# One more group of tiles turned by VectorE instead of TensorE, with its neighbours in the order moved

## The chip, the core and the metric

The kernel runs on one core of a Trainium2 chip. A core has TensorE for matrix products (and transposes, as products with the identity), VectorE, ScalarE and GpSimd for elementwise work, and SyncE, which issues all transfers here. The metric is the device time of one execution in microseconds.

## The reference

Two graph layers on x (16 graphs of 1024 nodes, 256 features, float32) with an int32 adjacency of 1024 x 1024 for each graph:

```
h = relu(layernorm(x));  Q, K, V = h Wq + bq, h Wk + bk, h Wv + bv   (8 heads of 32)
A = softmax(where(adj == 0, -inf, Q K^T / sqrt(32)));   x = x + (A V) Wo + bo
h = relu(layernorm(x));  e_k = leaky_relu((h * a_k) h^T, 0.2)   for k = 0..3
s = where(adj == 1, e_0, -9e15); where(adj == 2, e_1, s); ...;  x = x + softmax(s) h
```

With the inputs given, the adjacency holds only 0 and 1, so only e_0 is ever chosen; the kernel has branches for the other kinds that are skipped here.

## The kernel before

**Stages, slots, groups.** One stage handles the attention of one graph b, and in its background the second layer of graph b - 1 and the front of graph b + 1 (its norm, transposes, query and key products). There are 16 stages: stage 0 and stage 15 are written out, 1 to 14 are one loop. A stage has 64 slots, one for each tile: tile t = 4g + h is head h of a half of the heads, with 128 query rows; g is the group, 0 to 15, and four tiles make a group. Each engine has its own program, written in the order of the slots, and all meet by counters (semaphores). An engine runs its program strictly in order.

**What a tile needs.** TensorE makes the scores into `ps` (L1205, three slots ahead), VectorE adds the mask and takes the row minimum (L870, two slots ahead), ScalarE takes the exponential in place in `sm` (L595, one slot ahead), then the tile has to be transposed, 128 x 1024, and the four transposed tiles of a group are multiplied by V (`values`, L1236).

**Two ways to transpose.** In a *plain* tile TensorE makes eight 128 x 128 transposes into `pT` (L1217) and ScalarE and VectorE copy a half each into a home in `pt` (L606, L894). In a *swapped* group (`SWAPPED`, groups 3 to 9 before) tiles h = 0 and 1 are *turned*: VectorE transposes their 32 x 32 blocks into `turned` (L882), SyncE sends the blocks to a bounce buffer in HBM by eight transfers and back into homes 0 and 1 of `pt` by two (`swap_blocks`, L333 to L345). Tiles 2 and 3 of such a group stay plain, and ScalarE copies both halves (L606, L610). `turned` lies where the query and key weights lie; these are parked in `ks` at the start and brought back by `restore` (four transfers, L325) once a stage, after the last exchange and before the next front's query products.

**Homes.** `pt` has five. `place(t)` gives the home of a tile, `edge_place(t)` that of a row tile of the second layer. One edge tile, `SPARED` (6 before), lives in `spare`, which shares its memory with `parts`.

**The background.** `background` lists by slot the products that share the banks `pG`: values, edge products, edge sums, front transposes, query and key products. TensorE waits before each until the product two places earlier in that list is evacuated (`released`). The second layer has eight row tiles: two edge products in slots 13 + 4t and 14 + 4t (L1150 with `parts`), the masks of VectorE (L993), leaky relu (L1001), ScalarE's exponential (L655), TensorE's transposes `edge_transposes` (L1283) in slot 16 + 4t, the copies (L660, L1009) and the sums with h (L1292), then `result` (L1017).

**The masks.** SyncE loads a mask row tile as two halves `adj_half` (L279); GpSimd makes the bias of it (L505 for the next graph, L522 for the second layer), and ScalarE counts in `most_kind` (L630) whether other kinds occur, in slots 43, 46, 48, 51, 55, 58 and 61 for the next graph. `most_kind` waits for both halves, and the next load waits for it. On ScalarE it stands in the middle of everything else.

**The front.** VectorE takes statistics (L781), aggregates (L787), GpSimd raises to the power -1/2 (L528), VectorE makes the shift (L837), ScalarE normalises in four pieces (L644, slots 41 to 44). Query and key products go to `parts`, from which `first_stacks` sends twelve transfers (L299) for each of key and query.

Of the kernel before, what the change touches and what calls it, by code (L numbers as in the profile page):

```python
# [14 lines left out]
P = 128  # L15
B, N, D, H = 16, 1024, 256, 8
HD = D // H
NT = N // P
KT = D // P
HG = P // HD  # L20
# [14 lines left out]
SWAPPED = tuple(range(3, 10))  # L35
# [3 lines left out]
SPARED = SWAPPED[-1] + 1 - (EDGE // HG + 1)  # L39
LATE = tuple(t for t in range(NT) if EDGE // HG + 1 + t in SWAPPED)  # L40
# [20 lines left out]
def result_slot(t):  # L61

    return EDGE + 1 + 4 * NT if t == NT - 1 else EDGE + (8 if t in LATE else 7) + 4 * t

# [43 lines left out]
def place(t):  # L108


    g, h = t // HG, t % HG
    if g in SWAPPED:
        return h
    return 3 + (g + 1) % 2 if h == 0 else h - 1
# [12 lines left out]
def two_graph_layers(nc, x, adj, wq, bq, wk, bk, wv, bv, wo, bo, a_cols, y):  # L127
    ctx = ExitStack()
    with ctx:
# [98 lines left out]
        g_a, g_e, g_sel, g_chain = sem("g_a"), sem("g_e"), sem("g_sel"), sem("g_chain")  # L228
        def edge_home(t, c):

            if t == SPARED:
                return spare[:, c, 0:HALF].rearrange("p (m n) -> p m n", n=P)
            return pt[:, edge_place(t), NT // 2 * c:NT // 2 * (c + 1), :]
# [20 lines left out]
        def _(sp):  # L254
# [48 lines left out]
            def first_stacks(f, q):  # L303

                sp.wait_ge(qk_h, 8 * f + 2 * q + 2)
                settle(sp)
                sp.wait_ge(qk_l, 8 * f + 2 * q + 2)
                settle(sp)
                for head in range(HG):
                    stack(head, q)  # L310
# [58 lines left out]
            def stage(b, later):  # L369
# [34 lines left out]
                store(o, 4)  # L404
                if later:
                    mask_adj(b + 1, 0, base)
                    restore(b)
# [13 lines left out]
                if later:  # L421
                    mask_adj(b + 1, 3, base)
                    first_stacks(b + 1, 0)
                    mask_adj(b + 1, 4, base)
                    first_stacks(b + 1, 1)
                    mask_adj(b + 1, 5, base)
                    mask_adj(b + 1, 6, base)
# [33 lines left out]
            for t in range(NT - 1):  # L461
                if t == 1:
                    swap_blocks(0, 9)
                    restore(0)
                if t == 1:
                    sp.wait_ge(f_tr, 8)
                    settle(sp)
                    load_x1(0)
                sp.wait_ge(most_made, NT + t)
                settle(sp)  # L470
                load_adj(1, t, NT + t)
                if t == 3:
                    first_stacks(1, 0)
                if t == 4:
                    first_stacks(1, 1)
# [16 lines left out]
        def _(pool):  # L492
# [48 lines left out]
            def stage(b, later):  # L541
                o, base = b - 1, LOADS * b
                next_masks(b, NT - 1)
                layer_rstd(o)
                for t in range(NT):
                    if later and t == NT - 1:
                        front_rstd(b + 1)
                    edge_bias(o, t, base + t, NT * (b + 1))
                if later:
                    for node in range(5):  # L550
                        next_masks(b + 1, node)
                residual(b)
                if later:
                    for node in range(5, NT - 1):
                        next_masks(b + 1, node)
# [20 lines left out]
        def _(act):  # L576
# [21 lines left out]
            def copy(b, t, first):  # L598
                act.wait_ge(tr[0], len(PLAIN) * b + plain_before(t) + 1)
                if t % HG and (t >= HG or not first):  # L600
                    act.wait_ge(av, GROUPS * b + t // HG)
# [4 lines left out]
                nc.scalar.copy(pt[:, place(t), 0:NT // 2, :], pT[0][:, :].rearrange("p (m n) -> p m n", n=P)  # L606
                               ).then_inc(pt_made[0], 1)
                if t // HG in SWAPPED:
                    act.wait_ge(tr[1], len(PLAIN) * b + plain_before(t) + 1)
                    nc.scalar.copy(pt[:, place(t), NT // 2:, :], pT[1][:, :].rearrange("p (m n) -> p m n", n=P)  # L610
                                   ).then_inc(pt_made[1], 1)
# [51 lines left out]
            def stage(b, earlier, later):  # L663
# [36 lines left out]
                for s in range(TILES):  # L700
# [24 lines left out]
                    if later and s in (41, 42, 43, 44):  # L725
                        front_norm(b + 1, s - 41)
# [37 lines left out]
        def _(dve):  # L764
# [121 lines left out]
            def copy(b, t, first):  # L886
                dve.wait_ge(tr[1], len(PLAIN) * b + plain_before(t) + 1)
                if t % HG and (t >= HG or not first):
                    dve.wait_ge(av, GROUPS * b + t // HG)
# [4 lines left out]
                nc.vector.tensor_copy(pt[:, place(t), NT // 2:, :],  # L894
# [125 lines left out]
            def stage(b, earlier, later):  # L1020
# [26 lines left out]
                for s in range(TILES):  # L1047
                    for t in range(NT - 1):
                        if earlier and s == result_slot(t):
                            result(o, t, pG[bank("sum", t)])  # L1050
                    if s + 2 < TILES:
# [7 lines left out]
                    if earlier and EDGE + 4 <= s < EDGE + 4 + 4 * NT and (s - EDGE) % 4 == 0:  # L1059
                        t = (s - EDGE - 4) // 4  # L1060
                        edge_copy(o, t)
# [10 lines left out]
                    for kind, n in ahead[s]:  # L1072
                        if kind == "edge":
                            evacuate(kind, n)
                    if s in TURNED:
# [16 lines left out]
                    if later and s in (34, 38, 39):  # L1092
                        for n in {34: (3,), 38: (2,), 39: (0, 1)}[s]:
                            front_stats(b + 1, n)
                    if later and s == 40:
                        front_aggregate(b + 1)
                        front_shift(b + 1)
# [39 lines left out]
        def _(pe):  # L1137
# [83 lines left out]
            def values(b, g, i):  # L1221
# [7 lines left out]
                for m in range(NT):  # L1229
                    for h in range(HG):  # L1230
# [3 lines left out]
                        else:  # L1234
                            moving = pt[:, place(HG * g + h), m, :]
# [235 lines left out]
```

## Time and profile before

| | |
|---|---|
| median of 3 runs | 3695.5 us (3694.56 to 3705.17) |
| the profiled execution | 3700.19 us, its span 3698.4 us |
| granted clock of TensorE, mean | 0.972 of full |
| TensorE matmul, weight load | 3289.2 us (89%), 2715.2 us (73%) |
| VectorE, ScalarE, GpSimd | 2818.1 us (76%), 2448.6 us (66%), 1112.7 us (30%) |
| transfers of SyncE's queue | 538.36 MB, 52.9% of 16 engines' span |
| VectorE's copy of half a plain tile (L894) | 576 of them, mean 686 ns |

A busy share is an average over the whole span. Matmul records overlap, so the mean of one (279 ns for a 128 x 128 transpose) is longer than its part of the time: eight in a row take about 0.9 us from the first start to the next instruction's. In a timeline the bracket at the end of a line gives how long the engine stood idle just before and what ended it.

### The profile page before, as it was taken

What the parts mean: (1) busy time and instruction counts of PE and PEld (TensorE: products, weight loads), DVE (VectorE), ACT (ScalarE), POOL (GpSimd) and SP (SyncE); (2) the same over time, 40 slices, a digit from 0 to 9 for tenths busy, and PEclk for the clock granted to TensorE, in tenths of its full rate; (3) what the DMA queues carried; (4) which work ended last, traced back from release to release, by engine and by line L of the source; (5) the groups of instructions that cost most, each with busy time, mean ns of one, the idle gap of its engine ahead of it and who ended that gap; (6) DMA issues with size and microseconds to landing.
All of it is one profiled execution on the core that took longest, in us unless ns stands there. A gap on an engine that the chain in (4) does not pass through costs nothing. (4 is left out here: it accounts for less than half of the span.)

```text
span 3698.4 us, 96789 instructions
## 1 busy us (share of the span) xinstructions
PE 3289.2 (89%) x32304; PEld 2715.2 (73%) x32304; DVE 2818.1 (76%) x5398; ACT 2448.6 (66%) x4548; POOL 1112.7 (30%) x568
## 2 busy tenths in 40 slices
PE   5789989999998999999998998999999999998975
PEld 4577777777777787777777777777777777777854
DVE  4678777787878878777787878778787787877752
ACT  4677766767667677766767667676666767676641
POOL 1232323324223342322324233242322324232212
PEclk9899999999999999999999999999999999999987
DMA  5745546465454755546475454646545475554511
GB/s 132 207 123 156 159 124 180 127 197 139 134 168 122 206 136 167 153 122 173 128 209 144 130 170 125 194 130 177 150 130 166 123 212 143 156 160 113 157 33 39
DMA packets 331133, 546.84 MB, mean 148 GB/s; under 512 B 44480, under 2 KB 209600, under 8 KB 328384
## 3 DMA queue, kind: packets, MB, share of 16 engines
q1 hardware_dynamic: 330432, 538.36, 52.9%
q8 instruction: 334, 5.47, 0.6%
q14 instruction: 367, 3.01, 0.3%
HBM read 286.53 MB, written 134.22 MB: 114 GB/s over the span
## 5 line engine op out<-in xcount | busy, mean ns | idle before, releaser
L870 DVE CUSTOM_DVE_ANT_0 sm<-ps,bias 128x1024 f32<-128x1024 f32 x1024 | 1246.3, 1217 | 72.4 <-issue 28.5
L595 ACT ACTIVATE sm<-sm,mn 128x1024 f32<-128x1024 f32 x1024 | 1179.2, 1152 | 82.1 <-DVE mn L870 81.2
L1217 PE MATMUL pT<-ident,sm 128*128 128x128 f32 x6400 | 867.5, 279 | 147.3 <-ACT pt L606 111.0
L1217 PEld LDWEIGHTS pT<-ident,sm 128*128 128x128 f32 x6400 | 732.7, 142 | 327.6 <-ACT pt L606 159.7
L606 ACT COPY pt<-pT 128x512 f32<-128x512 f32 x800 | 465.1, 581 | 642.6 <-PE pT L1217 500.1
L522 POOL TENSOR_SCALAR gbias<-adj_half 128x512 bf16<-128x512 int32 x256 | 492.8, 1925 | 1195.3 <-DVE mn L993 906.4
L1205 PE MATMUL ps<-ks,qs 96*128 96x512 f32 x2048 | 752.5, 449 | 86.4 <-DVE mn L870 82.7
L505 POOL TENSOR_SCALAR bias<-adj_half 128x512 bf16<-128x512 int32 x256 | 492.5, 1924 | 785.6 <-DMA adj_half<-in_adj_dram 729.0
L894 DVE COPY pt<-pT 128x512 f32<-128x512 f32 x576 | 395.3, 686 | 267.0 <-PE pT L1217 200.9
L1236 PE MATMUL pG<-pt,v 128*32 128x128 f32 x16384 | 529.6, 284 | 26.3 <-DVE pt L894 19.6
L1236 PEld LDWEIGHTS pG<-pt,v 128*32 128x32 f32 x16384 | 456.0, 114 | 109.6 <-issue 87.7
L1205 PEld LDWEIGHTS ps<-ks,qs 96*128 96x128 f32 x2048 | 348.3, 193 | 185.0 <-DVE mn L870 143.1
L1292 PE MATMUL pG<-h,pt 128*128 128x256 f32 x1680 | 409.2, 379 | 0.0
L1150 PE MATMUL pG<-hh,parts 128*128 128x512 f32 x1024 | 382.6, 416 | 9.2 <-DVE x L1017 6.5
L993 DVE CUSTOM_DVE_ANT_0 sm<-pG,gbias 128x512 f32<-128x512 f32 x256 | 176.6, 690 | 219.0 <-PE pG L1150 174.0
L1292 PEld LDWEIGHTS pG<-h,pt 128*128 128x128 f32 x1680 | 308.7, 189 | 43.4
L882 DVE STREAM_TRANSPOSE turned<-sm 128x1024 f32<-128x1024 f32 x224 | 277.8, 1240 | 0.0
L655 ACT ACTIVATE sm<-sm,mnl 128x1024 f32<-128x1024 f32 x128 | 146.9, 1148 | 156.0 <-DVE mnl L1004 155.9
L1150 PEld LDWEIGHTS pG<-hh,parts 128*128 128x128 f32 x1024 | 199.2, 195 | 61.0 <-DVE x L1017 16.6
L1283 PE MATMUL pT<-ident,sm 128*128 128x128 f32 x1024 | 143.4, 286 | 83.0 <-ACT sm L655 66.1
L1150 PE MATMUL pG<-hh,wqk 128*128 128x512 f32 x512 | 192.9, 419 | 14.4 <-DVE hl L795 8.0
L1150 PE MATMUL pG<-hl,parts 128*128 128x512 f32 x512 | 205.6, 402 | 0.0
(102 smaller groups left out, 3617.6 us busy)
## 6 DMA issues: line engine op xcount, KB each, us to landing
adj_half<-in_adj_dram SPq DMA_DIRECT2D x512, 256.0 KB, 3.6
bounce<-turned SPq DMA_DIRECT2D x896, 128.0 KB, 2.5
pt<-bounce SPq DMA_DIRECT2D x224, 512.0 KB, 4.6
ks<-parts SPq DMA_DIRECT2D x384, 128.0 KB, 2.6
qs<-parts SPq DMA_DIRECT2D x384, 128.0 KB, 2.8
x<-in_x_dram SPq DMA_DIRECT2D x16, 1024.0 KB, 5.8
out_dram<-x SPq DMA_DIRECT2D x128, 128.0 KB, 4.6
wqk<-ks SPq DMA_DIRECT2D x60, 256.0 KB, 4.7
```

The lines of the kernel that those rows point to most:

```text
L505: nc.gpsimd.tensor_scalar(bias[:, node, c * HALF:(c + 1) * HALF], adj_half[:, c, :], 0.0, BIG, ALU.is_equal, ALU.mult).then_inc(adj_used[c ...
L522: nc.gpsimd.tensor_scalar(half, adj_half[:, c, :], 0.5, BIG, ALU.is_lt, ALU.mult).then_inc(adj_used[c], 1)
L595: nc.scalar.activation(sm[:, ring(t), :], sm[:, ring(t), :], ACT.Exp, scale=-1.0, bias=mn[:, t:t + 1], accum_out=den[:, t:t + 1]).then_inc ...
L606: nc.scalar.copy(pt[:, place(t), 0:NT // 2, :], pT[0][:, :].rearrange("p (m n) -> p m n", n=P)).then_inc(pt_made[0], 1)
L870: nc.vector.tensor_tensor_reduce(out=sm[:, ring(t), :], in0=ps[t % 2][:, :], in1=bias[:, node, :], scale=1.0, scalar=3e38, op0=ALU.add, op ...
L882: nc.vector.transpose(turned[:, t % HG, :, :, :].rearrange("p c m j -> p m c j"), sm[:, ring(t), :].rearrange("p (m c j) -> p m c j", m=NT ...
L894: nc.vector.tensor_copy(pt[:, place(t), NT // 2:, :], pT[1][:, :].rearrange("p (m n) -> p m n", n=P)).then_inc(pt_made[1], 1)
L1150: last = nc.tensor.matmul(out, a, c, start=start and i == 0, stop=stop and i == len(terms) - 1)
L1205: last = nc.tensor.matmul(ps[t % 2][:, c * HALF:(c + 1) * HALF], qs[0:ROWS, head, node * P:(node + 1) * P], ks[0:ROWS, head, c * HALF:(c + ...
L1217: last = nc.tensor.transpose(pT[c][:, j * P:(j + 1) * P], sm[:, ring(t), m * P:(m + 1) * P], ident[:, :])
L1236: last = nc.tensor.matmul(pG[i][HD * h:HD * (h + 1), 0:P], v[:, m, o:o + HD], moving, start=(m == 0), stop=(m == NT - 1))
L1292: last = nc.tensor.matmul(out[:, 0:D], edge_home(t, m // 4)[:, m % 4, :], h1[:, m, :], start=(m == 0), stop=(m == NT - 1))
```

## The change

`SWAPPED` becomes 3 to 10, so tiles 40 and 41 are turned too. From it follow: `SPARED` becomes 7, `LATE` gains edge tile 6, and the values of group 10 move from behind slot 44 to ahead in slot 46. Tile 45 (`ASIDE`) would take home 0 while group 10's exchanged tile is there, so it gets a home of its own beside the spared edge tile (`tile_home`). The parity in `place` follows the last swapped group. The front's statistics, aggregate and shift on VectorE and its norm on ScalarE are spread a slot later; the power on GpSimd comes behind the last edge bias instead of ahead of it. SyncE exchanges group 10, then restores the weights, then loads the first mask of the next graph, which stood ahead of the restore; and the query stacks are sent two heads before the sixth mask load and two behind it.

SyncE, after the exchange of group 9, in the loop (bounce and pt<-bounce are an exchange, wqk<-ks the restore, adj_half the mask). Before:

```order
L345 DMA pt<-bounce 128x1024 [waits bounced1]
L357 ISA [waits y_made]
L357 DMA out_dram<-x 128x256
L291 ISA
L279 ISA [waits g_sel,adj_used0]
L279 DMA adj_half<-in_adj_dram 128x512
L279 ISA [waits adj_used1]
L279 DMA adj_half<-in_adj_dram 128x512
L350 REGISTER_ALU
L325 DMA wqk<-ks 32x2048 [waits bounced0,bounced1]
L325 DMA wqk<-ks 32x2048 x3
```

Now:

```order
L344 DMA bounce<-turned 32x4x256 [waits turn_made]
L344 DMA bounce<-turned 32x4x256 x3
L348 REGISTER_ALU
L353 DMA pt<-bounce 128x1024 [waits bounced0,av]
L353 DMA pt<-bounce 128x1024 [waits bounced1]
L358 REGISTER_ALU
L333 DMA wqk<-ks 32x2048 [waits bounced0,bounced1]
L333 DMA wqk<-ks 32x2048 x3
L299 ISA
L287 ISA [waits g_sel,adj_used0]
L287 DMA adj_half<-in_adj_dram 128x512
L287 ISA [waits adj_used1]
```

The mask load moved from ahead of the restore to behind an exchange and the restore.

ScalarE, from the norm in slot 43 to tile 44's copy, before (gbias,most is the mask count, mnl the exponential of edge 7):

```order
L644 ACTIVATE rb<-rb,nmr,rstd 128x256
L625 REGISTER_ALU
L630 ACTIVATE gbias,most<-adj_half,mhalf 128x1024 [waits l_masked,adj_in1,adj_in0]
L594 REGISTER_ALU
L595 ACTIVATE sm,den<-sm,mn 128x1024 [waits masked]
L654 ISA
L655 ACTIVATE sm,den<-sm,mnl 128x1024 [waits leaky]
L599 REGISTER_ALU
L605 REGISTER_ALU [waits av,tr0]
L606 COPY pt<-pT 128x512 [waits pv]
```

Now:

```order
L655 ACTIVATE x<-x,nmr,rstd 128x256 [waits f_nmr]
L655 ACTIVATE x<-x,nmr,rstd 128x256
L636 REGISTER_ALU
L641 ACTIVATE gbias,most<-adj_half,mhalf 128x1024 [waits l_masked,adj_in1,adj_in0]
L605 REGISTER_ALU
L606 ACTIVATE sm,den<-sm,mn 128x1024 [waits masked]
L665 ISA
L666 ACTIVATE sm,den<-sm,mnl 128x1024 [waits leaky]
L610 REGISTER_ALU
L616 REGISTER_ALU [waits av,tr0]
L617 COPY pt<-pT 128x512 [waits pv]
```

Only the piece that is normalised ahead of it is another (x for rb). The mask count keeps its slot, and everything for slot 44 is still behind it.

TensorE, slots 44 to 46. Before, the values of group 10 stood in slot 44 ahead of the first front transposes (ident,x):

```order
L1205 MATMUL ps<-ks,qs 128x512 x2
L1214 REGISTER_ALU
L1217 MATMUL pT<-ident,sm 128x128 x8
L1236 MATMUL pG<-pt,v 32x128 x32
L1317 REGISTER_ALU
L1154 ISA
L1157 MATMUL pG<-ident,x 128x128 x4
L1389 REGISTER_ALU
L1283 MATMUL pT<-ident,sm 128x128 x8
L1368 REGISTER_ALU
```

Now the values stand in slot 46, ahead of the sum of edge tile 7 (h,spare), which the last front transposes (ident,sq) follow at once:

```order
L1250 MATMUL pG<-pt,v 32x128 x32
L1228 REGISTER_ALU
L1231 MATMUL pT<-ident,sm 128x128 x8
L1333 REGISTER_ALU
L1306 MATMUL pG<-h,spare 128x256 x8
L1315 REGISTER_ALU
L1168 REGISTER_ALU
L1171 MATMUL pG<-ident,rb 128x128 x4
L1168 REGISTER_ALU
L1171 MATMUL pG<-ident,sq 128x128 x4
```

The values moved two slots back, and the sum of edge tile 7 now touches the last front transposes.

```diff
-SWAPPED = tuple(range(3, 10))
+SWAPPED = tuple(range(3, 11))
+ASIDE = HG * (SWAPPED[-1] + 1) + 1
-    return EDGE + 1 + 4 * NT if t == NT - 1 else EDGE + (8 if t in LATE else 7) + 4 * t
+    return EDGE + 2 + 4 * NT if t == NT - 1 else EDGE + (8 if t in LATE else 7) + 4 * t
-    return 3 + (g + 1) % 2 if h == 0 else h - 1
+    assert t != ASIDE
+    return 3 + (g + SWAPPED[-1]) % 2 if h == 0 else h - 1
+        def tile_home(t, c):
+            if t == ASIDE:
+                return spare[:, 2 + c, 0:HALF].rearrange("p (m n) -> p m n", n=P)
+            return pt[:, place(t), NT // 2 * c:NT // 2 * (c + 1), :]
...  SyncE, in the loop
                 swap_blocks(b, 9)
                 store(o, 4)
+                swap_blocks(b, 10)
                 if later:
+                    restore(b)
                     mask_adj(b + 1, 0, base)
-                    restore(b)
...
-                    first_stacks(b + 1, 1)
+                    first_stacks(b + 1, 1, range(2))
                     mask_adj(b + 1, 5, base)
+                    first_stacks(b + 1, 1, range(2, HG))
                     mask_adj(b + 1, 6, base)
...  GpSimd
                 for t in range(NT):
-                    if later and t == NT - 1:
-                        front_rstd(b + 1)
                     edge_bias(o, t, base + t, NT * (b + 1))
+                if later:
+                    front_rstd(b + 1)
...  ScalarE
-                    if later and s in (41, 42, 43, 44):
-                        front_norm(b + 1, s - 41)
+                    if later and s in (42, 43, 44, 45):
+                        front_norm(b + 1, s - 42)
...  VectorE
+                    if earlier and s == EDGE + 4 + 4 * SPARED:
+                        edge_copy(o, SPARED)
+                    if later and s == 42:
+                        front_shift(b + 1)
-                    if later and s in (34, 38, 39):
-                        for n in {34: (3,), 38: (2,), 39: (0, 1)}[s]:
-                            front_stats(b + 1, n)
-                    if later and s == 40:
+                    if later and s in (34, 38, 39, 40):
+                        front_stats(b + 1, {34: 3, 38: 2, 39: 0, 40: 1}[s])
+                    if later and s == 41:
                         front_aggregate(b + 1)
-                        front_shift(b + 1)
...  ScalarE and VectorE, copy
-                if t % HG and (t >= HG or not first):
+                if t % HG and t != ASIDE and (t >= HG or not first):
```

## Rows read from the trace of the kernel before

**Rows 1.** Groups by form: line, engine, operation, shapes, count, busy us, mean ns, idle before.

```profile
L595 ACT ACTIVATE sm<-sm,mn 128x1024 f32<-128x1024 f32 x1024 | 1179.2, 1152 | 82.1 <-DVE mn L870 81.2
L1217 PE MATMUL pT<-ident,sm 128*128 128x128 f32 x6400 | 867.5, 279 | 147.3 <-ACT pt L606 111.0 <-issue 29.4 <-ACT pt L660 5.0
L606 ACT COPY pt<-pT 128x512 f32<-128x512 f32 x800 | 465.1, 581 | 642.6 <-PE pT L1217 500.1 <-PE pG L1236 128.6 <-PE pG L1292 13.8
...
L644 ACT ACTIVATE x<-x,nmr,rstd 128x256 f32<-128x256 f32 x64 | 34.9, 598 | 11.5 <-DVE nmr L837 11.5
```

**Rows 2.** Timeline of TensorE: start us, duration us, instruction [idle before <- what ended it].

```profile
1669.72 0.71 PE L1205 MATMUL ps<-ks,qs 96*128 96x512 f32 x2
...
1682.47 0.71 PE L1205 MATMUL ps<-ks,qs 96*128 96x512 f32 x2
...
1719.88 0.75 PE L1205 MATMUL ps<-ks,qs 96*128 96x512 f32 x2
...
1729.39 1.06 PE L1217 MATMUL pT<-ident,sm 128*128 128x128 f32 x8 [2.06 <-issue]
...
1742.60 1.95 PE L1236 MATMUL pG<-pt,v 128*32 128x128 f32 x64
...
1744.98 1.04 PE L1283 MATMUL pT<-ident,sm 128*128 128x128 f32 x8
...
1755.88 0.49 PE L1150 MATMUL pG<-hh,wqk 128*128 128x512 f32 x1 [0.48 <-DVE hl L795]
...
1792.32 1.36 PE L1217 MATMUL pT<-ident,sm 128*128 128x128 f32 x8 [2.22 <-ACT pt L606]
```

**Rows 3.** Timeline of GpSimd: the powers of front (L528) and layer (L539).

```profile
1064.76 1.66 POOL L528 TENSOR_TENSOR rstd<-vpe,mhalf 128x8 f32<-128x8 f32 x1 [18.89 <-DVE vpe L790]
1163.15 1.67 POOL L539 TENSOR_TENSOR rstd<-vpe,mhalf 128x8 f32<-128x8 f32 x1 [11.43 <-DVE vpe L833]
...
1725.10 1.66 POOL L528 TENSOR_TENSOR rstd<-vpe,mhalf 128x8 f32<-128x8 f32 x1 [18.89 <-DVE vpe L790]
1824.61 1.67 POOL L539 TENSOR_TENSOR rstd<-vpe,mhalf 128x8 f32<-128x8 f32 x1 [13.89 <-DVE vpe L833]
...
2168.83 1.66 POOL L528 TENSOR_TENSOR rstd<-vpe,mhalf 128x8 f32<-128x8 f32 x1 [18.89 <-DVE vpe L790]
2265.54 1.67 POOL L539 TENSOR_TENSOR rstd<-vpe,mhalf 128x8 f32<-128x8 f32 x1 [12.22 <-DVE vpe L833]
```

**Rows 4.** Timeline of VectorE at slots 37, 39 and 40.

```profile
1713.28 1.24 DVE L882 STREAM_TRANSPOSE turned<-sm 128x1024 f32<-128x1024 f32 x1
...
1721.02 1.40 DVE L781 BATCH_NORM_STATS2 st<-x 128x6 f32<-128x256 f32 x4
...
1726.79 0.17 DVE L837 SCALAR_TENSOR_TENSOR nmr<-mv,rstd 128x8 f32<-128x8 f32 x1 [1.88 <-POOL rstd L528]
```

**Rows 5.** Timeline of ScalarE: the mask counts of slots 43 and 58.

```profile
1739.81 1.14 ACT L630 ACTIVATE gbias<-adj_half,mhalf 128x1024 bf16<-128x1024 int32 x1
...
1789.43 1.15 ACT L630 ACTIVATE gbias<-adj_half,mhalf 128x1024 bf16<-128x1024 int32 x1 [1.81 <-DMA adj_half<-in_adj_dram]
```

**Rows 6.** Timeline of SyncE's transfer issues: start us, duration of all issues, count.

```profile
1717.55 1.64 SPq L345 DMA_DIRECT2D pt<-bounce  x2
...
1731.59 3.56 SPq L325 DMA_DIRECT2D wqk<-ks  x4
...
1776.22 8.69 SPq L299 DMA_DIRECT2D qs<-parts  x12
1785.41 1.39 SPq L279 DMA_DIRECT2D adj_half<-in_adj_dram  x2
```

**Rows 7.** Stretches: us, busy of PE, PEld, DVE, ACT, POOL, clock, transfers.

```profile
1792.00:1796.00 4.00, 3.68 (x56) 3.17 (x60) 2.58 (x4) 2.46 (x5) 2.54 (x3) 0.63 0.62 178
2081.00:2090.00 9.00, 6.98 (x24) 5.13 (x28) 7.05 (x16) 5.61 (x10) 0.92 (x1) 0.62 0.76 232
```

**Rows 8.** Issues of the page: count, KB each, median us from issue to landing.

```profile
adj_half<-in_adj_dram SPq DMA_DIRECT2D x512, 256.0 KB, 3.6
```

More of the change, by code:

```diff
@@ L301, in stack, with first_stacks @@
                                  ).then_inc((k_stacked, q_stacked)[q][head], 16)
-            def first_stacks(f, q):
+            def first_stacks(f, q, heads=range(HG)):
                 sp.wait_ge(qk_h, 8 * f + 2 * q + 2)
@@ L308, in first_stacks @@
                 settle(sp)
-                for head in range(HG):
+                for head in heads:
                     stack(head, q)
@@ L463, in _ @@
                     swap_blocks(0, 9)
+                    swap_blocks(0, 10)
                     restore(0)
@@ L605, in copy @@
                     act.wait_ge(pv, NT * b - NT + AFTER_SUM.index(t) + 1)
-                nc.scalar.copy(pt[:, place(t), 0:NT // 2, :], pT[0][:, :].rearrange("p (m n) -> p m n", n=P)
+                nc.scalar.copy(tile_home(t, 0), pT[0][:, :].rearrange("p (m n) -> p m n", n=P)
                                ).then_inc(pt_made[0], 1)
@@ L609, in copy @@
                     act.wait_ge(tr[1], len(PLAIN) * b + plain_before(t) + 1)
-                    nc.scalar.copy(pt[:, place(t), NT // 2:, :], pT[1][:, :].rearrange("p (m n) -> p m n", n=P)
+                    nc.scalar.copy(tile_home(t, 1), pT[1][:, :].rearrange("p (m n) -> p m n", n=P)
                                    ).then_inc(pt_made[1], 1)
@@ L887, in copy @@
                 dve.wait_ge(tr[1], len(PLAIN) * b + plain_before(t) + 1)
-                if t % HG and (t >= HG or not first):
+                if t % HG and t != ASIDE and (t >= HG or not first):
                     dve.wait_ge(av, GROUPS * b + t // HG)
@@ L893, in copy @@
                     dve.wait_ge(pv, NT * b - NT + AFTER_SUM.index(t) + 1)
-                nc.vector.tensor_copy(pt[:, place(t), NT // 2:, :],
+                nc.vector.tensor_copy(tile_home(t, 1),
                                       pT[1][:, :].rearrange("p (m n) -> p m n", n=P)).then_inc(pt_made[1], 1)
@@ L1060, in stage @@
                         t = (s - EDGE - 4) // 4
-                        edge_copy(o, t)
+                        if t != SPARED:
+                            edge_copy(o, t)
                     if earlier and s == 2:
@@ L1234, in values @@
                         else:
-                            moving = pt[:, place(HG * g + h), m, :]
+                            moving = tile_home(HG * g + h, m // 4)[:, m % 4, :]
                         last = nc.tensor.matmul(pG[i][HD * h:HD * (h + 1), 0:P], v[:, m, o:o + HD], moving, start=(m == 0), stop=(m == NT - 1))
```

## The prediction

> **What bounds the kernel now.** I read the page first, then the groups by form, then GpSimd's timeline for the length of a stage, then TensorE's timeline through one stage, and last the timelines of VectorE, SyncE and ScalarE around each place where TensorE stood still. TensorE is busy 89% of the span, and the weight loads beside it 73%. The largest TensorE group is the transposes of the exponentials: 6400 of them [rows 1]. Between slots 16 and 39 TensorE does not stop: slot 24 begins at 1669.72 and slot 28 at 1682.47, so a turned group takes 12.75 us of pure TensorE work [rows 2]. What TensorE loses lies at three kinds of place, the same in every stage:
> - In slots 40 to 47 it waits six times, 5.0 us together (1.15, 2.06, 0.70, 0.27, 0.36, 0.48). The longest is 2.06 us at 1729.39 [rows 2]. It is labelled "issue", but the copy it needs from VectorE is behind the shift of the front's norm, and VectorE waits 1.88 us there for GpSimd's power [rows 3, 4].
> - In slot 60 it waits 2.22 us at 1792.32 for a ScalarE copy [rows 2]. ScalarE is late because at 1789.43 it waited 1.81 us for the sixth mask tile [rows 5]. That load was issued at 1785.41, right after twelve stack transfers that held SyncE for 8.69 us from 1776.22 [rows 6].
> - Lower clock: after that second wait the granted clock is 0.63 over 1792 to 1796 [rows 7]. From the front's power to the layer's power a stage takes 96.71 us where no clock drop falls in it, 98.39 with only one near slot 41, 99.51 with only one near slot 60 [rows 3]. So a drop costs about 1.7 and 2.8 us. In 3 us slices of the trace the first is there in ten of the 14 stages and the second in nine, on average 1.2 and 1.8 us a stage.
>
> **Sum, part by part.** All times are those of the stage whose front power is at 1725.10, where no clock drop falls at slot 41. I work the new schedule from 1719.88, where slot 40 begins [rows 2], with durations from start to start.
>
> *Fewer transposes.* Tiles 40 and 41 leave TensorE: 16 transposes. Eight take about 0.87 us from start to start, so 1.75 us a stage, all of it on the path. By the ends of its rows it could be 2 x 8 x 0.279 = 4.5 us, since the listed 279 ns overlap; I take 1.75 [rows 1]. ScalarE keeps four copies (tiles 42 and 43, both halves). VectorE loses four copies of 0.69 (the table of the profile) and gains two transposes of 1.24 [rows 4], nothing on balance.
>
> *VectorE up to the turn.* The front's statistics stood as four in a row at 1721.02 [rows 4]; now two of them stand there (0.7), then mask 42 (1.15), turn 40 (1.15, to 1724.0), two statistics (0.7), result 5 (0.55), mask 43 (1.15, to 1726.4), the copy of edge 6 (0.6), edge mask 14 (0.6), turn 41 (1.15) to 1728.8, and the aggregate. The power needs from 1725.10 to 1726.79 as before [rows 3, 4], so the shift now comes at 1731.5. The copy that stood behind it is now before it. The 2.06 us wait becomes one of 1.2 us, at the scores of slot 42 (they need mask 43), and the 1.15, 0.70 and 0.27 go. TensorE then runs slot 42 from 1726.5: scores, values of group 9, transposes, edge 15, a quarter of edge values to 1731.9; slot 43 to 1734.1; slot 44's scores, transposes (behind a copy, 1734.9), half an edge value and the first front transposes to 1737.85. There it stands at the transposes of edge 7, which in the kernel before began at 1744.98 [rows 2]. Up to here the change is 7.1 us ahead: this is what it would give if nothing took it back.
>
> *What takes it back.* These transposes need ScalarE's exponential of edge 7 and its copy of tile 44, and both are queued behind the mask count of slot 43, which reads the first mask tile of the next front. On SyncE that load now stands behind the exchange of group 10 and behind the four transfers that restore the weights; before, it stood ahead of both. The chain: turn 41 ends 1728.8. For group 9 the turn of tile 37 ended at 1714.44 (1713.28 plus 1.16), and the two loads back were issued by 1719.19 (1717.55 plus 1.64), 4.75 us after it [rows 4, 6]. So SyncE is free at 1733.55. The restore takes 3.56 to issue [rows 6]: 1737.4. The halves of the mask follow, the second at about 1738.3, and land 3.6 us later [rows 8]: 1741.9. ScalarE reaches the count at 1735.8: shift 1731.5, two norms 1.0, exponential 44 1.15, two copies 1.0, two norms 1.0 [rows 1]. Before, it started the count at 1739.81 without a wait [rows 5]. Now it waits some 6 us, then needs count 1.14, exponential 45 1.14, exponential of edge 7 1.14, copy 0.5, a start 0.2: TensorE goes on at 1746.1, after 8.2 us of standing. For the load's arrival I take both ends: 2.8 us if nothing is queued in front of it (1741.1), 4.7 us, as the restore's own pieces need (1743.0), and 3.6 as the middle.
>
> A rule of the Trainium skill bears on this, page "DMA: Bandwidth & Descriptors", section "Queues, rings and completion order": on each engine the descriptors of one issuing queue are consumed in ring order, though a later one can finish first. By that rule the mask waits for the restore's megabyte, which speaks for the late end, about 1 us a stage more than my value. No row here shows this order of transfers.
>
> *Slots 45 to 47.* The work from edge 7's transposes to the first query product took 1744.98 to 1755.88, 10.9 us, of which 0.84 were waits [rows 2]. The values of group 10 now stand in it, 64 records from 1742.60, 1.95 us long and 1.89 to the next start [rows 2], and the last front transposes need result 7, which now comes directly behind sum 7: 0.6 us. With 0.1 to 0.3 for others, 10.06 + 1.89 + 0.6 = 12.5. The query product begins at 1758.6, that is 2.7 us late.
>
> *Clock.* After 8 us of standing I expect the lower clock (1.2 GHz) in every stage, where waits of 2.06 us had it in ten of 14. A lower-clock stretch in this trace costs 1.7, 2.8 and, over 2081 to 2090 at 0.62, 9 x 0.38 = 3.4 us [rows 3, 7]. I take 2.5; the drop near slot 41 that it replaces gave 1.2. Net +1.3. The Trainium skill, "TensorE: Matmul & The Clock Gate", Part 1, says that the throttled state is the default and activity releases it; by that rule the drop is certain here, as in my sum, and no run yet shows it.
>
> *Stacks.* Only six query transfers now stand before the sixth mask (heads 0 and 1), so it is issued half of 8.69 = 4.3 us earlier by SyncE, limited by GpSimd's release to about 3.9. It lands near 1785.5, and ScalarE asks at 1787.6 [rows 5, 6]. The 1.8 us wait goes, and with it 1.8 of TensorE's 2.22. The other six transfers end by 1787, long before slot 61 needs them. The clock drop near slot 60 goes with it: 1.8 on average. The wait of 1.65 us for the fifth mask, behind the key stacks, stays.
>
> *Homes.* Other places in pt, the spare home for tile 45 and edge 7: same instructions and sizes. Nothing, bounds -0.2 to +0.2 us a stage, because only the order of waits changes.
>
> Sum a stage: +2.7 + 1.3 - 1.8 - 1.8 = +0.4. Over 14 looped stages +6 us; the first and last stage have no such load behind a restore and give 1.75 each, -4. Profiled: 3700.2 + 2 = 3702. The median shown is 4.7 below the profiled run, so 3698.
>
> **Rivals.**
> 1. *The load is in time.* If the mask tile lands at or before 1735.8, TensorE continues at 1739.9 and not 1746.1 and keeps its clock: 0.4 - 6.2 - 2.5 = -8.3 a stage, 14 x 8.3 = 116, with the 4 of the outer stages 120, time 3576. It needs 6 us less on a chain of issues that are all in the trace. Half of it, a load 3 us earlier at the same clock, is 0.4 - 3.1 = -2.7 a stage and gives 3653. For it: the stores and exchange can be faster here, since fewer loads run beside them. Against: every issue has its row. Chance 0.20 for 3576 to 3660.
> 2. *The standing costs more clock than I give it (slower).* Place: slots 44 to 47 behind edge 7. If TensorE is at the lower level from its restart up to the query product, more than 5 us, it costs the 3.4 us of 2081 to 2090 and not 2.5, and with the load at 4.7 us (+1.1) the stage is +2.4, 14 x 2.4 = 34, less 4: 3725. If in addition the next stretch drops again (2.8) it is +5.2: 3765. It decides from a standing of about 10 us, or from two low stretches a stage. Chance 0.20.
> 3. *The change is hidden.* Slots 40 to 47 are bound by ScalarE and SyncE and not by TensorE, the stack gain is eaten by the load for slot 61: within 3 us of before, 3695. Chance 0.05.
>
> **How the numbers follow.** The forecast, 3698, has 0.55, own range 3665 to 3735: 1 us more or less on the load and 1 us on the clock are 14 us each, and either of the two gains can fail by half. Of it 0.17 is faster by over 0.3% (11 us, about what a measurement of this kernel tells from no change), 0.19 within, 0.19 slower. With rival 1 faster has 0.37, with rival 3 the middle 0.24, with rival 2 slower 0.39. The range reaches to half of either rival: 3625 to 3750.
>
> **What would show it.** Right: ScalarE's count of slot 43 waits some 5 to 7 us for adj_half in each looped stage, TensorE's transposes of edge 7 wait some 8 us with a clock near 0.5 behind them, VectorE's wait for the power is under 1 us and holds nobody, the sixth mask has no wait and the clock is 1.00 in slots 60 to 62. TensorE has 6144 transposes on that line. Wrong: no wait at that count (rival 1), or a waiting adj_half at slot 58 still (the stack term is lost, +3.6 a stage).

## The result, and the profile after

The changed kernel takes 3810.89 us (median of 4 runs, 3798.64 to 3816.13), the kernel before 3695.03 on the same chip (3693.89 to 3705.17): 1.0303 times, interval 1.027 to 1.0335. It is slower by 3%, outside the predicted range. The profiled execution took 3816.13 us, its span is 3814.3, the mean granted clock 0.947 after 0.972.

The page after: TensorE, the transposes of the exponentials, those of the second layer, ScalarE's mask counts, the instruction queue, and the landing of masks and restored weights.

```profile
PE 3286.5 (86%) x32048; PEld 2714.4 (71%) x32048; DVE 2819.8 (74%) x5366; ACT 2446.3 (64%) x4548; POOL 1112.7 (29%) x568
...
q8 instruction: 345, 5.65, 0.7%
...
L1231 PE MATMUL pT<-ident,sm 128*128 128x128 f32 x6144 | 839.3, 280 | 71.7 <-ACT pt L617 68.7
...
L1297 PE MATMUL pT<-ident,sm 128*128 128x128 f32 x1024 | 157.9, 305 | 234.0 <-ACT pt L617 170.3
...
L641 ACT ACTIVATE gbias<-adj_half,mhalf 128x1024 bf16<-128x1024 int32 x128 | 146.7, 1146 | 170.0 <-DMA adj_half<-in_adj_dram 168.1
...
adj_half<-in_adj_dram SPq DMA_DIRECT2D x512, 256.0 KB, 4.1
...
wqk<-ks SPq DMA_DIRECT2D x60, 256.0 KB, 6.9
```

The 256 transposes are gone from the first group ([rows 1] had 6400), and its own idle time has halved. It has gone elsewhere: 170.3 us before the transposes of the second layer, and 168.1 us of ScalarE waiting for masks. One instruction queue moved 345 pieces; in the page of before this row reads `334, 5.47, 0.6%`, for a longer TensorE program. The prediction does not use that row.

TensorE in the stage whose front power is at 2011.00, and its jump back to the loop's top in the stage before (start, duration, instruction, [idle before]).

```profile
1860.57 1.09 PE L1231 MATMUL pT<-ident,sm 128*128 128x128 f32 x8 [0.32 <-ACT pt L617]
1864.86 1.19 PE L1219 MATMUL ps<-ks,qs 96*128 96x512 f32 x2 [3.20 <-issue]
...
2001.19 0.75 PE L1219 MATMUL ps<-ks,qs 96*128 96x512 f32 x2
...
2007.78 0.73 PE L1219 MATMUL ps<-ks,qs 96*128 96x512 f32 x2 [1.08 <-DVE mn L881]
...
2032.03 1.97 PE L1297 MATMUL pT<-ident,sm 128*128 128x128 f32 x8 [12.65 <-ACT pt L617]
...
2044.11 0.65 PE L1171 MATMUL pG<-ident,sq 128*128 128x128 f32 x4 [0.30 <-DVE x L1028]
2045.86 0.48 PE L1164 MATMUL pG<-hh,wqk 128*128 128x512 f32 x1
...
2080.48 1.09 PE L1231 MATMUL pT<-ident,sm 128*128 128x128 f32 x8 [0.30 <-ACT pt L617]
```

This answers [rows 2]. Slot 40 starts at 2001.19. The 2.06 us wait has become one of 1.08, and the 2.22 us wait of slot 60 is one of 0.30. Two waits are new: 12.65 us ahead of edge 7's transposes, and 3.20 us at the jump back to the top of the loop, behind the last transposes of the iteration. Over the 14 looped stages the first is 11.2 to 13.4 us long (12.1 on average). The second is over 3 us in 11 of the 13 jumps between them.

VectorE's second turn and its shift, ScalarE's counts of slots 43 and 58, and SyncE's issues.

```profile
2008.85 1.24 DVE L893 STREAM_TRANSPOSE turned<-sm 128x1024 f32<-128x1024 f32 x1
...
2012.70 0.17 DVE L848 SCALAR_TENSOR_TENSOR nmr<-mv,rstd 128x8 f32<-128x8 f32 x1 [0.47 <-POOL rstd L539]
```

```profile
2028.01 1.15 ACT L641 ACTIVATE gbias<-adj_half,mhalf 128x1024 bf16<-128x1024 int32 x1 [10.94 <-DMA adj_half<-in_adj_dram]
...
2077.60 1.14 ACT L641 ACTIVATE gbias<-adj_half,mhalf 128x1024 bf16<-128x1024 int32 x1
```

```profile
2005.47 6.52 SPq L344 DMA_DIRECT2D bounce<-turned  x8
2012.25 2.16 SPq L353 DMA_DIRECT2D pt<-bounce  x2
2014.66 3.43 SPq L333 DMA_DIRECT2D wqk<-ks  x4
2018.51 2.14 SPq L287 DMA_DIRECT2D adj_half<-in_adj_dram  x2
...
2065.24 4.38 SPq L307 DMA_DIRECT2D qs<-parts  x6
2071.30 1.19 SPq L287 DMA_DIRECT2D adj_half<-in_adj_dram  x2
2072.69 3.74 SPq L307 DMA_DIRECT2D qs<-parts  x6
```

These answer [rows 4 to 6]. The order of issues is as predicted and its times are near: the mask's second half is out by 2020.65. But ScalarE gets the tile at 2028.01, and the transfers issued between 2018.4 and 2020.7 have this median from issue to landing:

```profile
adj_half<-in_adj_dram SPq DMA_DIRECT2D x2, 256.0 KB, 8.5
```

That is 8.5 us where [rows 8] has 3.6. This stage is on the late side: over the 14 looped stages the 28 halves land 6.2 to 9.0 us after their issue, median 7.6. In each of these stages they land 0.3 to 1.2 us behind the last piece of the restore (here at 2027.29 and 2027.93, the restore's last at 2026.91). ScalarE waits 9.4 to 11.7 us for them, 10.4 on average. The clock (columns as in [rows 7]) at the restart, behind it, and in slots 58 to 61:

```profile
2033.00:2036.00 3.00, 3.00 (x16) 2.70 (x15) 1.96 (x4) 2.06 (x4) 2.70 (x2) 0.58 0.36 122
2036.00:2040.00 4.00, 4.00 (x81) 3.41 (x80) 3.02 (x6) 3.60 (x7) 0.87 (x1) 1.00 0.01 4
2071.00:2080.00 9.00, 8.62 (x79) 6.77 (x70) 6.75 (x12) 8.04 (x17) 8.76 (x4) 1.00 0.60 149
```

TensorE goes on at 0.50 in the first 3 us behind the restart in all 14 stages, which is its lower level of 1.2 GHz. From 4 to 8 us behind it the clock is 1.00 in the stage shown and between 0.72 and 1.00 in the others.

**Where a stage's time went.** I took the starts of VectorE's 64 masks per stage from the timelines (mask s is taken two slots before slot s) and averaged over ten looped stages. us from the first to the second mask named:

| masks | before | after | split alone | reorder | mask first | mask first, padded |
|---|---|---|---|---|---|---|
| 0 to 4 | 13.29 | 17.84 | 13.30 | 13.29 | 17.28 | 13.38 |
| 4 to 40 | 122.67 | 122.46 | 123.14 | 123.08 | 122.90 | 122.50 |
| 40 to 50 | 44.16 | 51.66 | 44.16 | 41.10 | 39.57 | 39.57 |
| 50 to 60 | 26.56 | 26.58 | 26.70 | 26.89 | 26.52 | 26.85 |
| 60 to next 0 | 13.85 | 11.05 | 11.11 | 11.10 | 11.08 | 11.10 |
| stage | 220.53 | 229.59 | 218.41 | 215.46 | 217.35 | 213.40 |

The last four columns are experiments below. The changed kernel's stage is 9.06 us longer: +4.55 behind the jump, +7.5 around edge 7, -2.8 at slot 60, -0.2 in between.

### The profile page after: what moved, and what is told of

Read it like the earlier page. It is cut to its first block and busy times, and to the rows that moved or that the text cites. A ratio compares the mean times of both kernels' runs of the same rounds, so it can differ in the third digit from the quotient of the medians.

```text
span 3814.3 us, 96121 instructions
## 1 busy us (share of the span) xinstructions
PE 3286.5 (86%) x32048; PEld 2714.4 (71%) x32048; DVE 2819.8 (74%) x5366; ACT 2446.3 (64%) x4548; POOL 1112.7 (29%) x568
## 5 line engine op out<-in xcount | busy, mean ns | idle before, releaser
L1231 PE MATMUL pT<-ident,sm 128*128 128x128 f32 x6144 | 839.3, 280 | 71.7 <-ACT pt L617 68.7
L1231 PEld LDWEIGHTS pT<-ident,sm 128*128 128x128 f32 x6144 | 711.6, 143 | 239.8 <-ACT pt L617 113.9
L617 ACT COPY pt<-pT 128x512 f32<-128x512 f32 x752 | 437.0, 581 | 554.2 <-PE pT L1231 553.0
L905 DVE COPY pt<-pT 128x512 f32<-128x512 f32 x496 | 340.2, 686 | 217.8 <-PE pT L1231 199.8
L1297 PE MATMUL pT<-ident,sm 128*128 128x128 f32 x1024 | 157.9, 305 | 234.0 <-ACT pt L617 170.3
L1297 PEld LDWEIGHTS pT<-ident,sm 128*128 128x128 f32 x1024 | 131.9, 156 | 264.2 <-ACT pt L617 173.9
L893 DVE STREAM_TRANSPOSE turned<-sm 128x1024 f32<-128x1024 f32 x256 | 317.4, 1240 | 0.0
L641 ACT ACTIVATE gbias<-adj_half,mhalf 128x1024 bf16<-128x1024 int32 x128 | 146.7, 1146 | 170.0 <-DMA adj_half<-in_adj_dram 168.1
```

The costliest lines, as they stand in the source:

```text
L617: nc.scalar.copy(tile_home(t, 0), pT[0][:, :].rearrange("p (m n) -> p m n", n=P)).then_inc(pt_made[0], 1)
L905: nc.vector.tensor_copy(tile_home(t, 1), pT[1][:, :].rearrange("p (m n) -> p m n", n=P)).then_inc(pt_made[1], 1)
L1231: last = nc.tensor.transpose(pT[c][:, j * P:(j + 1) * P], sm[:, ring(t), m * P:(m + 1) * P], ident[:, :])
L1297: last = nc.tensor.transpose(pT[c][:, j * P:(j + 1) * P], sm[:, RING, m * P:(m + 1) * P], ident[:, :])
```

## The experiments

Each has its ratio to the kernel before on the same chip, which took 3697.62, 3703.84 and 3703.41 us in the three groups.

**Theory:** the mask load lands late behind the exchange and the restore. **Rivals:** only the issue order on SyncE makes it late; the new order of front and homes costs time itself; the split brings the wait at the jump.

### The mask load first, or between

```diff
+                if later:
+                    mask_adj(b + 1, 0, base)
                 swap_blocks(b, 10)
                 if later:
                     restore(b)
-                    mask_adj(b + 1, 0, base)
```

> The changed kernel with one thing moved on SyncE: the first mask load of the next graph is issued ahead of the exchange of group 10 and of the restore. Theory 1 (the late mask load is the loss): ScalarE's count of slot 43 waits for nothing, TensorE's transposes of edge 7 wait about 2 us in place of 12, the lower clock behind them goes; 10 + 1.7 us a stage, 14 stages, 165 us less than the changed kernel: 3646. Rival (ScalarE or VectorE is late there for another reason, or the exchange of group 10 itself is late for the values in slot 46): TensorE still stands over 6 us in slots 44 to 46, time above 3730.

Measured: 3646.97 us, ratio 0.9873 [0.9854, 0.9893]. TensorE's waits (us in all, number, longest):

```profile
PE ps L1220 <- DVE mn L882: 107.8, 135, 4.1
...
PE pT L1298 <- ACT pt L618: 23.5, 15, 1.6
```

The standing at edge 7 is 1.6 us in place of 12, and the kernel is faster than the changed one and the one before. So the place of this one load is worth some 160 us here, as was expected (3646). The wait at the jump is still there (9 of 13 times over 3 us).

In the second kernel the load stands between the exchange and the restore (`swap_blocks(b, 10)`, `mask_adj(b + 1, 0, base)`, `restore(b)`).

> The changed kernel with the first mask load between the exchange of group 10 and the restore. It is issued 3.4 us earlier than in the changed kernel. If only SyncE's issue order counts, ScalarE's wait falls from 10.4 to 7 us a stage and the time to 3763. If the load also waits on the transfer engines behind the restore's 1 MB, as theory 1 has it, it falls to some 3 us (landing 3.6 us after issue) and the time to about 3700.

Measured: 3764.22 us, ratio 1.0177 [1.0152, 1.0202]. TensorE stands 6.4 to 8.2 us a looped stage at edge 7:

```profile
PE pT L1297 <- ACT pt L617: 103.5, 15, 8.2
```

With 12.1 behind both, some 7 behind the exchange alone and 1.6 ahead of both, about 5 us are due to the restore and 5 to 6 to the exchange. The 3700 that the theory gave missed. It took the load to land 3.6 us after its issue once the restore is behind it; the halves take 5.5 to 8.1 us here, median 6.7, for the exchange is still ahead of them. The 3763 of the issue order alone is met in number and not in kind: the restore's four issues take 3.4 us, and having them ahead costs 5. The next but one experiment changes the bytes and keeps the order.

### The split, taken out and alone

```diff
-                    first_stacks(b + 1, 1, range(2))
+                    first_stacks(b + 1, 1)
                     mask_adj(b + 1, 5, base)
-                    first_stacks(b + 1, 1, range(2, HG))
```

> The changed kernel with the twelve query transfers in one piece ahead of the sixth mask load again. Theory: the split is worth the wait of slot 60 (2.2 us and a lower clock in most stages), but the new wait of 3.2 to 3.8 us at the jump back to the loop's start, in 11 of 14 stages, appears because that wait is gone; then without the split the wait at the jump goes and the time stays within 15 us of the changed kernel. Rival: the wait at the jump comes from something else in the change (homes, longer TensorE program); then it stays, slot 60 waits again, and the time is 3811 + 14 x 3.6 = 3861.

Measured: 3835.63 us, ratio 1.0374 [1.0353, 1.0395]. All 13 jumps have a wait of 2.8 to 3.9 us, so the split does not cause it. The loss is 25 us and not the 50 of the rival: without the split the stage is 0.9 us longer at slot 60 and 1.2 us behind the jump (masks 60 to next 0 and 0 to 4, over the stages of the table).

> The kernel before with only the split of the query stack (two heads ahead of the sixth mask load, two behind). If the split alone brings the wait at the jump, it gives 2.2 + 1.8 and costs 2.9 + 1.5 a stage: within 15 us of before. If the wait at the jump has another cause: 3.6 us a stage less, 3645.

Measured (the kernel before, with the split alone): 3667.73 us, ratio 0.9923 [0.9903, 0.9942]. The split is worth 25 us in the new order and 30 in the old, some 2 us a stage and not the 3.6 expected; by the table it gives 2.7 at slot 60 in the old order and loses 0.5 between masks 4 and 40. There is no long wait at its jump.

### Fewer bytes ahead of the mask

```diff
+                    most = 1 if g == 10 else 4
-                    sp.dma_start(pt[:, h, :, :].rearrange("p m n -> p (m n)"),
-                                 bounce[half, :, :, h, :, :].rearrange("c j a w -> (c j) (a w)")).then_inc(swapped, 16)
+                    sp.dma_start(pt[:, h, 0:2 * most, :].rearrange("p m n -> p (m n)"),
+                                 bounce[half, :, :, h, 0:most, :].rearrange("c j a w -> (c j) (a w)")
+                                 ).then_inc(swapped, 16)
```

This version leaves three quarters of the two exchanged tiles of group 10 as they were, so its result is not the reference's.

> The changed kernel, whose exchange of group 10 brings back only a quarter of each of its two tiles (128 KB in place of 512 KB each; the rest of the two tiles is left from the group before, so the values of group 10 are not the reference's). The order of SyncE's queue, the waits and every other transfer stay. Theory A: the mask load lands 8 to 9 us after its issue because some 1 MB of the exchange and 1 MB of the restored weights are still being moved ahead of it at about 210 GB/s; 768 KB less brings it about 3.6 us earlier, TensorE stands 8 to 9 us at edge 7 in place of 12, and the kernel takes 3811 - 14 x 3.6 = 3760. Theory B: the landing is late for another reason than the bytes ahead (the fixed chain of issues on SyncE): it stands 11 to 12.5 us as before, 3800 to 3815.

Measured: 3759.71 us, ratio 1.0153 [1.0114, 1.0192]. TensorE stands 8.0 to 8.7 us a looped stage, mean 8.3. Its waits, and the median landing of the transfers issued in 1762 to 1768:

```profile
PE pT L1299 <- ACT pt L619: 117.2, 15, 8.7
```

```profile
adj_half<-in_adj_dram SPq DMA_DIRECT2D x2, 256.0 KB, 4.4
```

The landing is 4.4 us, with the same transfers in the same order; over the 28 halves of the looped stages the median is 4.4 for the 7.6 of the changed kernel. 768 KB less ahead bring 12.1 - 8.3 = 3.8 us of standing, as expected, which is 207 GB/s; between 2016 and 2018 the changed kernel's DMA engines moved 227 GB/s in all. So the load waits for the bytes queued ahead of it. The Trainium skill, "DMA: Bandwidth & Descriptors", section "Queues, rings and completion order", has the descriptors of a queue consumed in ring order on each engine; the trace agrees with it: in the changed kernel the mask's halves land behind the restore's last piece in all 14 stages, 0.3 us or more.

### Empty instructions ahead of TensorE's loop

What was left was the wait at the jump: up to here in every kernel with group 10 turned, in none without. In the trace of the version with the mask load first, the instruction queue moves a piece of 16 KB from 1768.2 to 1769.2 while TensorE stands (from 1767.8), and TensorE goes on at 1771.17. So it is with each of the nine long waits: a piece starts to move within 0.5 us of the start of the wait. What the 2 us between the piece's end and TensorE's next instruction are spent on, no run shows. The Trainium skill, "Runtime: NRT & Kernel Launch", section "Instruction fetch mechanics", says that instructions come in 16 KB blocks of 256 and that a taken branch to a target outside the window held forces a fetch. If so, the place of the loop in the blocks decides.

```diff
                 last.then_inc(w_tr, 1)
+            for _ in range(64):
+                settle(pe)
```

`settle` adds to a counter that nobody reads. The other two versions have 128 and 192 of them.

> The version with the mask load first, and 64 empty instructions (semaphore increments that nobody waits for) on TensorE once, before its first stage. In that version's trace TensorE stands 3.0 to 3.5 us at the first scores of 9 of its 13 loop iterations, and each time a 16 KB piece of its instructions is moved by the instruction queue just before it goes on. Theory A: what it waits for is a piece of its own program, and whether the piece is there in time depends on where the loop's first and last instruction lie in the pieces. 64 instructions shift them all; with one of the shifts of 64, 128 and 192 the number of standing iterations should change to 0 to 3, or to 13. Each is worth some 4.5 us with its clock, so near 3647 - 9 x 4.5 = 3607 where none is left, 3665 with all 13. Theory B: the fetch is merely late behind the key stack transfers that SyncE issues just then, wherever the loop lies: 8 to 11 standing iterations in each of the three, 3647 to 3655. The empty instructions themselves may cost up to 3 us once.

> As with 64, but 128 empty instructions before the loop. Theory A: a count of standing iterations that is clearly another than 9 in at least one of the three shifts, with the time following at 4 to 5 us for each. Theory B: 8 to 11 of them here too, 3647 to 3656.

> As with 64, but 192 empty instructions before the loop. Theory A as there. Theory B: 8 to 11 standing iterations here too, 3647 to 3658.

Measured: 3593.4 us, ratio 0.97 [0.9679, 0.9722]; 3595.49, ratio 0.9718 [0.9698, 0.9738]; 3618.3, ratio 0.9775 [0.9757, 0.9793] (its first front power is 10 us late, and masks 4 to 40 take 0.9 us a stage longer than with 64, for a reason that no run shows). No jump in any of the three has a wait of 1 us. The 3593.4 is below the 3607 expected, because the jumps without a long wait had lost something too, as the masks show below. The 64-instruction version at one jump, and the instruction queue's row of its page:

```profile
1754.79 1.09 PE L1234 MATMUL pT<-ident,sm 128*128 128x128 f32 x8 [0.44 <-ACT pt L618]
1755.82 1.95 PE L1253 MATMUL pG<-pt,v 128*32 128x128 f32 x64
1757.70 1.99 PE L1203 MATMUL pG<-wot,ot 128*128 128x256 f32 x8
```

```profile
q8 instruction: 333, 5.46, 0.7%
```

345 pieces without the 64 instructions, 333 with them: about one less for each of 13 jumps. Masks 2 to 4 take 5.9 us in all 13 iterations, and 6.4 to 11.4 in the unpadded version: every iteration lost something, 3.9 us on average. The traces agree with the rule on fetches as far as the pieces go, about one more for each jump; which instruction decides it they don't show.

**Controls.** The same 64 instructions behind the loop; 64 ahead of the loop of the changed kernel itself; 224 ahead of the loop of the kernel before.

> The version with the mask load first, with 64 empty instructions on TensorE behind its loop, ahead of the last stage. Nothing before or in the loop moves. Theory A: the waits at the jump are there as without them, in 8 to 11 of 13 iterations, 3645 to 3655. If the empty instructions did it in another way than by the place of the loop, they go and the time falls towards 3593.

Measured: 3660.09 us, ratio 0.9889 [0.9867, 0.9911], 345 pieces. Six jumps have waits over 3 us, fewer than the 8 I named; masks 2 to 4 take 6.7 to 12.9 us in all 13. So the empties do not help by being there. Behind the loop they cost some 9 us once, and the time is 5 us above the expected range. TensorE ahead of the last stage:

```profile
3295.47 1.19 PE L1220 MATMUL ps<-ks,qs 96*128 96x512 f32 x2 [9.29 <-issue]
```

> The changed kernel as it is, with 64 empty instructions on TensorE once before its loop. Theory A (a piece of TensorE's own program comes late at the jump back when the loop lies badly in the pieces; 64 instructions further it does not): the 11 waits of 3.0 to 3.8 us at the jump go, the 12 us of standing at edge 7 stay, and the time falls by about 11 x 4.9 = 54 us to 3757. Theory B (what the shift mended is tied to the version with the mask load first): 3800 to 3815, with waits at the jump in 9 or more iterations.

Measured: 3772.66 us, ratio 1.0197 [1.0172, 1.0222]. The waits at the jump are gone, 4.5 us a stage between masks 0 and 4. The standing at edge 7 is 12.5 us on average for 12.1, masks 40 to 50 take 0.5 us longer and masks 50 to 60 0.3. Of the 54 us expected, 38 came.

> The kernel before, with 224 empty instructions on TensorE before its loop, which puts the loop's first instruction where it would lie in a 256-instruction piece with 32 fewer, as the 16 transposes that the change takes out of the first stage (with their weight loads) do. Its end is then 32 behind where the changed kernel's is. Theory A: the kernel before catches the wait at the jump in some of its 13 iterations, up to 4.9 us each: 3705 to 3770 where it stood at 3704 on this chip. Theory B (the wait belongs to the changed order): none, 3695 to 3715. In both, the empty instructions cost about 10 us once, before the first stage, as 192 of them did (its first front power came at 192.05 us in place of 181.74).

Measured: 3722.13 us, ratio 1.0051 [1.0036, 1.0065]. Its row of the queue, and TensorE behind two jumps:

```profile
q8 instruction: 347, 5.69, 0.7%
```

```profile
1390.02 1.19 PE L1207 MATMUL ps<-ks,qs 96*128 96x512 f32 x2 [3.44 <-DVE mn L870]
...
2282.75 0.41 PE L1238 MATMUL pG<-pt,v 128*32 128x128 f32 x5
2284.10 1.94 PE L1238 MATMUL pG<-pt,v 128*32 128x128 f32 x59 [0.94 <-issue]
```

13 pieces more, and masks 2 to 4 take 6.8 to 7.7 us in twelve of the jumps and 11.7 in one, where the kernel before has 5.9 to 6.0 in all. The kernel before catches the same loss from a shift alone, though mostly in its short form. The time alone would not show it: in the profiled execution the empties cost 19.8 us at the start (first front power 197.40 for 177.60), as much as the whole difference of the medians. That execution is also the longest of its seven, 3738.92 us.

### The new order without the turned group

```diff
-SWAPPED = tuple(range(3, 11))
+SWAPPED = tuple(range(3, 10))
...
-                swap_blocks(b, 10)
                 if later:
+                    mask_adj(b + 1, 0, base)
                     restore(b)
-                    mask_adj(b + 1, 0, base)
...
-                    swap_blocks(0, 10)
```

> The changed kernel with groups 3 to 9 turned, as before, and without the two exchanges of group 10; the mask load is issued ahead of the restore as before; the later front, the homes and the split query transfers stay. TensorE's program has the length that it had before, so by theory A no wait at the jump. My prediction put the later front at +2.7 us a stage in slots 45 to 47 and +1.3 of clock: with that it would take 3668 (the kernel before with the split alone) + 14 x 1.5 to 4 = 3690 to 3725. If the later front costs nothing, or takes TensorE's stand at VectorE's shift away without giving it back, 3630 to 3670.

Measured: 3631.29 us, ratio 0.9812 [0.9789, 0.9835], 334 pieces. The later front is a gain: 44.16 to 41.10 us between masks 40 and 50, in place of the loss that the expectation allowed for. It differs from the split alone, which has 44.16 there, in the later slots of the front and the small moves that go with them. TensorE waits once, at its last front transposes:

```profile
1712.62 0.66 PE L1169 MATMUL pG<-ident,sq 128*128 128x128 f32 x4 [2.16 <-DVE x L1026]
```

The turned group itself, with its mask load first and the loop padded, gives another 2.06 us a stage (215.46 to 213.40 in the table); the sum had 1.75 for its transposes.

## Why the prediction was wrong

- **Fewer transposes, VectorE up to the turn: right.** From slot 40's start I had ScalarE asking for the mask at +15.9 and TensorE standing from +18.0; measured +15.88 (2028.01 - 10.94 - 2001.19) and +18.19. VectorE's wait for the power is 0.47 us.
- **What takes it back: the place was right, the size was wrong.** The step that failed is "land 3.6 us later [rows 8]". 3.6 us is the median over 512 loads; this load had the exchange's 1 MB and the restore's 1 MB ahead of it and took 7.6 us (median), 8.5 in the stage shown. My upper bound of 4.7 was again a median, that of the restore's pieces, which themselves rose to 6.9. With that ScalarE waited 10.4 us on average for 6 and TensorE 12.1 for 8.2. I even cited the ring order and priced it at 1 us a stage. It should have been priced by bytes: exchange, restore and mask are 2.5 MB from 2012.25 on, at 200 to 230 GB/s an estimated 11.4 to 13.1 us, and the same load needed 2.6 us in the kernel before with nothing just ahead. That makes 2026.3 to 2028.0; it landed at 2027.93.
- **Slots 45 to 47 and the clock: nearly right.** From the restart to the query product 13.83 us passed in this stage and 14.4 on average over the 14 (13.7 to 15.1), where I had 12.5 and 2.5 of clock. The clock was low behind every restart, as forecast, and cost some 1.9 us (an estimate, 14.4 - 12.5).
- **Slots 40 to 50 together:** predicted +4.0 us, measured +7.5. Without the standing they would be -4.6 (mask first), so the late mask costs 12.1 us a stage.
- **Stacks: right in kind.** The wait for the sixth mask is gone and the clock is 1.00 there; -2.8 measured, -3.6 predicted; the split alone gave 2.1 a stage.
- **Homes: nothing, right as far as can be seen.** Masks 4 to 40 take the same time to 0.2 us. They were not tried alone.
- **The jump: missing, and the larger half of the error.** +4.55 us a stage, from no step of the change's schedule: the sum has no term for it. TensorE's program got shorter by the transposes and their weight loads, and its loop came to lie badly. Of the error of 8.7 us a stage this is 4.55; 3.5 are slots 40 to 50 with the late load, 0.8 the smaller stack gain, and -0.2 the rest. Neither error alone explains the miss: with the jump mended the changed kernel still takes 3772.66 us, and 13 x 4.55 us on top of the forecast would be 3757.
- **The rivals.** Rival 2 named the decisive point, a standing of about 10 us, which was reached; its mechanism, more lower clock, was not what cost: the clock took 1.9 us where it had 3.4. Rival 1 described what happens when the load is in time: 3576 to 3660, and with the mask load first the kernel took 3646.97, with the loop padded too 3593.4 to 3618.3.

**Open:** why most jumps of the unpadded new order lose about 4 to 5 us and some only 1, and why the kernel before, shifted, has the short form nearly always. Which instruction of the loop must lie where is not shown, so the place of the loop is shown as the cause and its mechanism, the fetch, is argued from the pieces.

## What to carry to other kernels

Price a transfer by the bytes ahead of it in its queue at the rate the queue has there, and what it takes alone on top, not by the median landing of its kind. Put the small load that an in-order engine waits for ahead of the big ones that nobody needs yet. When a change alters the length of a looped program, compare the instruction queue's count of pieces and read the first instructions behind the jump; if pieces were added, a few dozen empty instructions ahead of the loop may give the time back.

## What I had not expected of the hardware

- The place of a loop in TensorE's program is worth up to 50 us of 3600: 64 empty instructions took 3646.97 us to 3593.4 (ratios 0.9873 and 0.97), and spans 3640.8 to 3592.8.
- The wait is labelled "issue" or with the mask of VectorE that had ended, never with the instruction fetch. Only the queue's row shows it: 345 to 347 pieces with it, 333 or 334 without.
- Empty counter increments take time where nothing hides them, an estimated 0.14 us each: 64 behind the loop left TensorE idle for 9.29 us, and its idle time ahead of the first front transposes is 12.6 us with none, 12.3 with 64, 16.1 with 128 and 26.2 with 192.
- 256 KB took 8.5, 4.4 and 2.8 us to land, the last in the version with fewer bytes and with no other issue within 4 us ahead of it.
